# Packing the diagonal steps of causal attention into full score units

## The chip, the core and the metric

The kernel runs on one core of a Trainium2 chip. A core has five engines that run their own instruction streams and meet at semaphores: PE (TensorE, matrix products), DVE (VectorE) and ACT (ScalarE) for elementwise work, POOL (GpSimd), and SP, which here issues DMA transfers. PE writes only to PSUM, a small memory of eight banks of 128 partitions by 512 fp32 columns; the other tiles are in SBUF. The metric is the device time of one execution, in microseconds (us).

## The reference

Two transformer layers in a row; the change is in the attention of the first, over 4096 positions and 16 heads of 16 channels:

```python
scores = jnp.einsum('bhsd,bhtd->bhst', q, k) / math.sqrt(float(DH))
mask = jnp.tril(jnp.ones((S, S), dtype=scores.dtype))
scores = scores * mask
scores = jnp.where(scores == 0.0, -jnp.inf, scores)
attn = jax.nn.softmax(scores, axis=-1)
out = jnp.einsum('bhst,bhtd->bhsd', attn, v)
```

It is causal: query s sees keys t up to s. A score that is exactly 0 within the triangle is masked as well, so the kernel has to look at each score, not only at its place. Around it lie layer norms, the projections, a gated feed-forward, and in the second layer a linear-recurrence attention and a 16-expert feed-forward. None of that is touched.

## The kernel before

`phase_attend` does the attention as 32 blocks: 4 groups of 4 heads (g), and in each 8 blocks of 512 queries (j = 0 to 7). Block (g, j) has 4(j+1) steps, one for each tile of 128 keys (kt). A step's scores lie transposed, keys on partitions and queries along the columns. A step has two units, each of two heads: 128 x 1024 scores in two PSUM banks. `ps_s` holds three units.

For each unit PE makes the scores (L805, bf16), ACT takes exp of them into `probs` (L859), and DVE multiplies `probs` with "score is not 0" (L892, fp32), which also frees the unit's banks. In the second tile of every four below the diagonal ("shared" steps) one of the four heads goes another way: ACT copies its scores out (L864) and POOL does the comparison and the product (L904, L907). Then PE weighs the values of the whole step: four products of 32 output partitions, one for each head, in fp32 (L820), summed over the block's steps in `ps_o`. The sum of the weights comes with them as a further column of the values.

The last four steps of a block are the diagonal. In step d (0 to 3) only the queries from column 128 d on see its keys, so PE, ACT, DVE and the weighing work on 512, 384, 256 and 128 columns of each head (`w0 = 128 d`). In the first 128 of these columns, the square, the triangle cuts through: POOL sets what lies above it to 0 (L912, one instruction for the four heads), and the weighing waits for it (`masked`).

The order on PE is written out by hand: in step n it issues the scores of the step's second unit, then those of step n+1's first unit, then the weighing of step n-2. A unit's scores wait until DVE has done the unit three before (`bank`). `probs` has four slots, one for each step, so exp of step n waits for the weighing of step n-4. The end of block b is done inside block b+1's diagonal: ACT copies `ps_o` out in its step d=1 (L850), PE turns the copy over in step d=2 behind the weighing (L828, four transposes), and DVE normalises behind the last unit (L876 reciprocal, L880 product). Blocks with j = 0 do this a step later and leave normalising to the next block's first step. SP loads the queries of block b+1 as soon as the scores of block b-1 are all made (L755, eight transfers).

## Time and profile before

| | us |
|---|---|
| median of 3 runs | 2318.0 (2317.34 to 2320.04) |
| the profiled execution | 2317.24 |
| its span | 2315.5 |
| attention in it, first DVE instruction to last | 1286.87 (191.24 to 1478.11) |

Busy time over the span: PE 2003.0 us (87%), DVE 1665.2 (72%), ACT 1414.9 (61%), POOL 899.9 (39%). Such shares are means over stages with different limits. The page's row of tenths shows it: DVE at 9 in every slice from the fifth to the nineteenth, which is attention, and at 3 to 6 behind it. A group's "idle before" is time that the engine stood still just before these instructions, and what ended it. In a timeline each line has its start in us from the span's start, its length and its count. The next line can start a little before the end of the one before, since instructions of one engine overlap.

### The profile page before, as it was taken

Reading aid. Unit: us, or ns where it says so; the run is one execution under the profiler, and the core shown is the slowest. Engines: PE = TensorE matmul, PEld = TensorE weight load, DVE = VectorE, ACT = ScalarE, POOL = GpSimd, SP = SyncE. Lnnn points to the kernel's source line nnn. Section 1 sums busy time; section 2 is a strip of 40 time slices with the busy share of each in tenths; the row PEclk is TensorE's granted clock in tenths of the full one; section 3 lists DMA queues with packets and bytes.
Section 4 is the critical chain, followed back from the end, with each engine's and each line's share of the span. In section 5 each row is a group of like instructions: output and inputs, shape, how many; then the busy total and the mean of one; then the engine's idle time right before and its main releaser. Section 6 shows DMA issues by size and latency. Waiting matters only on the chain. (4 is left out here: it accounts for less than half of the span.)

```text
span 2315.5 us, 29427 instructions
## 1 busy us (share of the span) xinstructions
PE 2003.0 (87%) x10349; PEld 816.3 (35%) x10349; DVE 1665.2 (72%) x2280; ACT 1414.9 (61%) x1841; POOL 899.9 (39%) x777
## 2 busy tenths in 40 slices
PE   4986898988899988898989898678886699999997
PEld 4541111111111121111121111256553356767775
DVE  2776999999999999999999999556665544333332
ACT  0676888888888888888888888445554211111110
POOL 1682333333333333333333333126565174334334
PEclk8997999999999999999999999799998899999999
DMA  2463211102111112112530000110000043444441
GB/s 104 158 204 89 42 30 21 31 15 50 21 30 21 31 44 41 31 21 55 169 102 12 12 12 3 61 42 32 19 1 1 7 141 120 102 111 93 105 105 23
DMA packets 124646, 133.90 MB, mean 58 GB/s; under 512 B 35145, under 2 KB 118946, under 8 KB 123808
## 3 DMA queue, kind: packets, MB, share of 16 engines
q1 hardware_dynamic: 109920, 118.09, 18.9%
q0 software_dynamic: 14592, 14.08, 3.5%
q8 instruction: 77, 1.26, 0.2%
q14 instruction: 57, 0.47, 0.1%
HBM read 97.08 MB, written 50.63 MB: 64 GB/s over the span
## 5 line engine op out<-in xcount | busy, mean ns | idle before, releaser
L892 DVE SCALAR_TENSOR_TENSOR arena<-ps_s,arena 128x1024 f32<-128x1024 f32 (+3 forms) x1152 | 1163.1, 1076 | 114.5 <-ACT arena L859 108.1
L859 ACT ACTIVATE arena<-ps_s 128x1024 f32<-128x1024 f32 (+3 forms) x1152 | 1053.3, 959 | 192.7 <-PE ps_s L805 173.9
L805 PE MATMUL ps_s<-arena 128*128 128x512 bf16 (+3 forms) x2304 | 632.6, 367 | 145.1 <-DVE arena L892 98.8
L820 PE MATMUL ps_o<-arena,values 128*32 128x512 f32 (+3 forms) x4608 | 573.5, 570 | 0.4 <-POOL arena L912 0.4
L904 POOL TENSOR_SCALAR arena<-arena 128x512 f32<-128x512 f32 x112 | 215.0, 1919 | 611.1 <-ACT arena L864 611.1
L805 PEld LDWEIGHTS ps_s<-arena 128*128 128x128 bf16 x2304 | 143.1, 97 | 801.6 <-DVE arena L892 761.1
L1826 ACT ACTIVATE arena<-g_ps_g 128x320 f32<-128x320 f32 (+1 forms) x96 | 42.0, 438 | 311.0 <-PE g_ps_u L1760 311.0
L2011 POOL DMA_INDIRECT out<-values,slot_ids x80 | 123.8, 1547 | 240.7 <-DVE values L1975 212.4
L912 POOL TENSOR_SCALAR_AFFINE_SELECT arena<-arena 128x512 f32<-128x512 f32 x128 | 81.2, 635 | 239.2 <-DVE arena L892 239.2
L820 PEld LDWEIGHTS ps_o<-arena,values 128*32 128x32 f32 x4608 | 90.8, 108 | 224.8 <-issue 207.7
L1948 DVE TENSOR_TENSOR arena<-g_ps_u,arena 128x320 f32<-128x320 f32 (+1 forms) x96 | 47.2, 492 | 168.3 <-ACT arena L1826 168.3
L907 POOL TENSOR_TENSOR arena<-arena 128x512 f32<-128x512 f32 x112 | 142.6, 1274 | 9.3
L1253 PE MATMUL t_ps_out<-arena 128*128 128x256 f32 x512 | 126.8, 407 | 19.7 <-DVE arena L1483 8.8
L1760 PE MATMUL g_ps_g<-arena 128*128 128x320 f32 (+1 forms) x384 | 119.7, 434 | 0.6 <-issue 0.6
L1760 PE MATMUL g_ps_u<-arena 128*128 128x320 f32 (+1 forms) x384 | 120.1, 435 | 0.0
L1253 PEld LDWEIGHTS t_ps_out<-arena 128*128 128x128 f32 x512 | 103.7, 206 | 42.7 <-issue 19.9
L1775 PE MATMUL g_ps_d<-arena 128*128 128x256 f32 (+1 forms) x480 | 107.9, 381 | 1.1 <-DVE arena L1948 1.0
L1775 PEld LDWEIGHTS g_ps_d<-arena 128*128 128x128 f32 (+1 forms) x480 | 89.4, 189 | 15.3 <-DVE arena L1948 1.6
L1992 POOL DMA_INDIRECT slots_in_dram<-arena,scatter_at x64 | 70.3, 1099 | 55.0 <-issue 55.0
L1261 PE MATMUL t_ps_turn<-ident,arena 128*128 128x128 f32 x256 | 37.4, 294 | 52.2 <-ACT arena L1147 18.8
L1760 PEld LDWEIGHTS g_ps_u<-arena 128*128 128x128 f32 (+1 forms) x384 | 69.8, 182 | 34.5 <-issue 0.6
L1760 PEld LDWEIGHTS g_ps_g<-arena 128*128 128x128 f32 (+1 forms) x384 | 69.5, 181 | 33.2 <-issue 1.4
(201 smaller groups left out, 1780.7 us busy)
## 6 DMA issues: line engine op xcount, KB each, us to landing
arena<-parts_dram SPq DMA_DIRECT2D x320, 64.0 KB, 2.3
parts_dram<-arena SPq DMA_DIRECT2D x32, 384.0 KB, 2.9
arena<-parts_dram SPq DMA_DIRECT2D x24, 512.0 KB, 7.1
slots_in_dram<-in_empty_slots SPq DMA_DIRECT2D x10, 1040.0 KB, 25.5
arena<-slots_in_dram SPq DMA_DIRECT2D x16, 650.0 KB, 4.4
arena<-in_L_ffn_w_gate SPq DMA_DIRECT2D x16, 352.0 KB, 3.1
arena<-in_L_ffn_w_up SPq DMA_DIRECT2D x16, 352.0 KB, 3.7
arena<-in_L_attn_x SPq DMA_DIRECT2D x8, 512.0 KB, 3.9
```

The source lines that it names most:

```text
L805: last = pe.matmul(ps_s[:, u % 3, h, step.w0:], m.k_stack[:, head, step.kt * P:step.kt * P + P], q_stack[:, step.block % 2, 2 * pair + h, ...
L820: last = pe.matmul(ps_o[32 * h:32 * h + 32, step.block % 2, step.w0:], m.values_flat[:, at:at + 32], probs[:, step.slot, h, step.w0:], sta ...
L859: act.activation(probs[:, step.slot, 2 * pair:2 * pair + 2, step.w0:], ps_s[:, u % 3, :, step.w0:], ACT.Exp, scale=1.0 / DH ** 0.5).then_i ...
L892: dve.scalar_tensor_tensor(p, ps_s[:, u % 3, 0:heads, step.w0:], 0.0, p, ALU.not_equal, ALU.mult).then_inc(bank, 1)
L904: pool.tensor_scalar(s_copy, s_copy, 0.0, 0.0, ALU.is_equal, ALU.is_equal).then_inc(kept, 1)
L907: pool.tensor_tensor(p, p, s_copy, ALU.mult).then_inc(last_masked, 1)
L912: pool.affine_select(out=sq, in_=sq, compare_op=ALU.is_ge, fill=0.0, base=0, pattern=[[0, HG], [1, P]], channel_multiplier=-1).then_inc(ma ...
L1253: last = pe.matmul(ps_out[:, c, t * D:t * D + D], lhs[:, k, at:at + P], w[:, k], start=k == 0, stop=k == KC - 1)
L1760: last = pe.matmul(ps[0:rows_, n % 2, 0:HALF], w[:, s, k, at:at + rows_], inT[:, s, k, half * HALF:half * HALF + HALF], start=k == 0, stop ...
L1775: last = pe.matmul(ps_d[:, (s + i) % 2, at:at + D], hidden_e[0:rows_, s, f, c * P:c * P + P], w_down[0:rows_, s, f], start=f == 0, stop=f ...
L1992: pool.indirect_dma_start(out=m.slots_in[:, :], out_offset=bass.IndirectOffsetOnAxis(ap=m.scatter_at[:, k, t:t + 1], axis=0), in_=m.h_wide ...
L2011: pool.indirect_dma_start(out=out_rows, out_offset=bass.IndirectOffsetOnAxis(ap=ids[:, s, c:c + 1], axis=0), in_=rows_out[:, s, c], in_off ...
```

## The change

The four diagonal steps of a block, eight units of 1024, 768, 512 and 256 columns, become three steps with five units of 1024 columns each:

- "square": tile 4j, two full units, as step d=0 was.
- "mixed": tiles 4j+1 and 4j+3, two units. Each head's bank holds the 384 columns of the first and, in its last quarter, the 128 columns of the second.
- "half": tile 4j+2, one unit. The 256 columns of all four heads lie two to a bank.

The scores, exp and the product on DVE now always cover whole units. PE makes the same products as before, column for column, out of more places: the mixed step's unit takes four products (384, 384, 128, 128), the half step's takes four of 256. The weighing of the mixed step is eight instructions instead of four. POOL does two squares one after the other in the mixed step and one in each of the others, four in a block as before. A step now has one or two units, so units are counted on their own; the transposes stand in the half step, the copy in the mixed step (in the half step for j = 0), and normalising behind the half step's unit.

On PE the stretch around a diagonal (in a block with j = 2; the weighing of a step stands two steps behind its scores) read before:

```order
L820 MATMUL ps_o<-arena,values 32x512 x4
L805 MATMUL ps_s<-arena 128x384 x2
L805 MATMUL ps_s<-arena 128x256 x2
L820 MATMUL ps_o<-arena,values 32x512 x4
L805 MATMUL ps_s<-arena 128x256 x2
L805 MATMUL ps_s<-arena 128x128 x2
L820 MATMUL ps_o<-arena,values 32x512 x4
L828 MATMUL ps_o<-ident,arena 128x128 x4
L805 MATMUL ps_s<-arena 128x128 x2
L805 MATMUL ps_s<-arena 128x512 x2
L820 MATMUL ps_o<-arena,values 32x384 x4
L805 MATMUL ps_s<-arena 128x512 x4
```

and reads now:

```order
L853 MATMUL ps_o<-arena,values 32x512 x4
L836 MATMUL ps_s<-arena 128x384 x2
L836 MATMUL ps_s<-arena 128x128 x2
L836 MATMUL ps_s<-arena 128x256 x4
L853 MATMUL ps_o<-arena,values 32x512 x4
L836 MATMUL ps_s<-arena 128x512 x2
L853 MATMUL ps_o<-arena,values 32x512 x4
L861 MATMUL ps_o<-ident,arena 128x128 x4
L836 MATMUL ps_s<-arena 128x512 x4
L853 MATMUL ps_o<-arena,values 32x384 x4
L853 MATMUL ps_o<-arena,values 32x128 x4
L836 MATMUL ps_s<-arena 128x512 x4
```

The 384-column and 128-column scores of two steps have come together (second and third row), the half step's scores stand as four products in one unit, and between that unit and the transposes (L861) there are two weighings (rows with `ps_o<-arena,values`) with one pair of scores between them. The weighing of the mixed step is the pair of rows with 384 and 128 columns.

On DVE a block with j = 2 and the units of the next read before:

```order
L892 SCALAR_TENSOR_TENSOR arena<-ps_s,arena 128x1024 x7
L892 SCALAR_TENSOR_TENSOR arena<-ps_s,arena 128x512
L892 SCALAR_TENSOR_TENSOR arena<-ps_s,arena 128x1024 x6
L892 SCALAR_TENSOR_TENSOR arena<-ps_s,arena 128x2x384 x2
L892 SCALAR_TENSOR_TENSOR arena<-ps_s,arena 128x2x256 x2
L892 SCALAR_TENSOR_TENSOR arena<-ps_s,arena 128x2x128 x2
L876 RECIPROCAL arena<-ps_o 128x16
L880 TENSOR_TENSOR arena<-ps_o,arena 128x256
```

and read now:

```order
L926 SCALAR_TENSOR_TENSOR arena<-ps_s,arena 128x1024 x7
L926 SCALAR_TENSOR_TENSOR arena<-ps_s,arena 128x512
L926 SCALAR_TENSOR_TENSOR arena<-ps_s,arena 128x1024 x9
L910 RECIPROCAL arena<-ps_o 128x16
L914 TENSOR_TENSOR arena<-ps_o,arena 128x256
```

The six narrower products are gone, three full ones are there in their place (9 in a run, of which 5 are the diagonal's), and the normalising of the previous block stands behind the fifth.

The diff, without the lines that only follow from these:

```diff
+class Piece:
+
+
+    def __init__(self, head, kt, w0, bank, at, width):
+        self.head, self.kt, self.w0 = head, kt, w0
+        self.bank, self.at, self.width = bank, at, width
...
 class Step:
 
 
-    def __init__(self, n, g, j, kt):
-        self.n, self.g, self.j, self.kt = n, g, j, kt
+    def __init__(self, n, g, j, kind, kt, unit):
+        self.n, self.g, self.j, self.kind, self.kt = n, g, j, kind, kt
...
-        self.diag = kt - TT * j if kt >= TT * j else None
-        self.last = self.diag == TT - 1
-        self.w0 = P * self.diag if self.diag else 0
-        self.shared = self.diag is None and kt % 4 == 1
-
-    def unit(self, pair):
-
-        return 2 * self.n + pair
+        self.last = kind == "half"
+        self.shared = kind == "full" and kt % 4 == 1
+        self.pairs = 1 if kind == "half" else 2
+        self.unit = unit
+        self.squares = {"full": 0, "square": 1, "mixed": 2, "half": 1}[kind]
+
+    def pieces(self, pair):
+
+
+        if self.kind == "half":
+            return [Piece(h, self.kt, 2 * P, h // 2, h % 2 * 2 * P, 2 * P) for h in range(HG)]
+        heads = [(2 * pair + h, h) for h in range(2)]
+        if self.kind == "mixed":
+            return [Piece(head, self.kt, P, h, 0, 3 * P) for head, h in heads] + \
+                   [Piece(head, self.kt + 2, 3 * P, h, 3 * P, P) for head, h in heads]
+        return [Piece(head, self.kt, 0, h, 0, BT) for head, h in heads]
+
+    def last_unit(self):
+        return self.unit + self.pairs - 1
 
...
-        return self.block * TT + self.diag + 1
...
+        return self.block * TT + {"square": 0, "mixed": 1, "half": 3}[self.kind] + self.squares
...
+def block_kinds(j):
+
+    return [("full", kt) for kt in range(TT * j)] + [("square", TT * j), ("mixed", TT * j + 1), ("half", TT * j + 2)]
 
...
 BLOCKS = NG * NB
...
-    if step.diag == (1 if step.j else 2) and step.block:
+    if step.kind == ("mixed" if step.j else "half") and step.block:
         return step.block - 1
...
-    if step.diag == (2 if step.j else 3) and step.block:
+    if step.kind == "half" and step.block:
         return step.block - 1
...
-    if step.j and step.diag == 3:
+    if step.j and step.kind == "half":
         return step.block - 1
...
-                    sp.wait_ge(scored, 2 * steps_through(b - 2))
+                    sp.wait_ge(scored, units_through(b - 2))
...
-                for h in range(2):
-                    head = step.g % 2 * HG + 2 * pair + h
-                    last = pe.matmul(ps_s[:, u % 3, h, step.w0:], m.k_stack[:, head, step.kt * P:step.kt * P + P],
-                                     q_stack[:, step.block % 2, 2 * pair + h, step.w0:], start=True, stop=True)
+                for p in step.pieces(pair):
+                    last = pe.matmul(ps_s[:, u % 3, p.bank, p.at:p.at + p.width],
+                                     m.k_stack[:, step.g % 2 * HG + p.head, p.kt * P:p.kt * P + P],
+                                     q_stack[:, step.block % 2, p.head, p.w0:p.w0 + p.width], start=True, stop=True)
                 last.then_inc(scored, 1)
...
-                for h in range(HG):
-                    at = (step.kt * NH + step.g * HG + h) * (DH + 1)
-                    last = pe.matmul(ps_o[32 * h:32 * h + 32, step.block % 2, step.w0:], m.values_flat[:, at:at + 32],
-                                     probs[:, step.slot, h, step.w0:], start=step.first, stop=step.last,
-                                     tile_position=(0, 32 * h))
+                pieces = [(pair, p) for pair in range(step.pairs) for p in step.pieces(pair)]
+                for pair, p in sorted(pieces, key=lambda entry: (entry[1].kt, entry[1].head)):
+                    at = (p.kt * NH + step.g * HG + p.head) * (DH + 1)
+                    last = pe.matmul(ps_o[32 * p.head:32 * p.head + 32, step.block % 2, p.w0:p.w0 + p.width],
+                                     m.values_flat[:, at:at + 32], probs[:, step.slot, 2 * pair + p.bank, p.at:p.at + p.width],
+                                     start=step.first, stop=step.last, tile_position=(0, 32 * p.head))
                 last.then_inc(probs_free, 1)
...
-                    score(step, 1)
+                    if step.pairs == 2:
+                        score(step, 1)
...
-                    for pair in range(2):
-                        u = step.unit(pair)
+                    for pair in range(step.pairs):
+                        u = step.unit + pair
                         act.wait_ge(scored, u + 1)
-                        act.activation(probs[:, step.slot, 2 * pair:2 * pair + 2, step.w0:], ps_s[:, u % 3, :, step.w0:], ACT.Exp,
+                        act.activation(probs[:, step.slot, 2 * pair:2 * pair + 2], ps_s[:, u % 3], ACT.Exp,
                                        scale=1.0 / DH ** 0.5).then_inc(exped, 1)
...
-                    for pair in range(2):
-                        u = step.unit(pair)
+                    for pair in range(step.pairs):
+                        u = step.unit + pair
                         dve.wait_ge(exped, u + 1)
...
-                        p = probs[:, step.slot, 2 * pair:2 * pair + heads, step.w0:]
-                        dve.scalar_tensor_tensor(p, ps_s[:, u % 3, 0:heads, step.w0:], 0.0, p, ALU.not_equal, ALU.mult).then_inc(bank, 1)
...
-                    if step.diag is not None:
-
-                        pool.wait_ge(bank, step.unit(1) + 1)
-                        sq = probs[:, step.slot, :, step.w0:step.w0 + P]
-                        pool.affine_select(out=sq, in_=sq, compare_op=ALU.is_ge, fill=0.0, base=0,
-                                           pattern=[[0, HG], [1, P]], channel_multiplier=-1).then_inc(masked, 1)
+                    if step.squares:
+
+                        pool.wait_ge(bank, step.last_unit() + 1)
+                        if step.kind == "half":
+                            heads = probs[:, step.slot, 0:2].rearrange("p b (h n) -> p (b h) n", h=2)
+                        else:
+                            heads = probs[:, step.slot]
+                        for c in range(step.squares):
+                            sq = heads[:, :, 3 * P * c:3 * P * c + P]
+                            pool.affine_select(out=sq, in_=sq, compare_op=ALU.is_ge, fill=0.0, base=0,
+                                               pattern=[[0, HG], [1, P]], channel_multiplier=-1).then_inc(masked, 1)
```

## Rows read from the trace of the kernel before

**Rows 1.** Busy time by stretch: one diagonal, one block with j = 0, all of attention.

```profile
core 0: us, PE busy (x) PEld busy (x) DVE busy (x) ACT busy (x) POOL busy (x), PEclk, DMA share, GB/s
1011.06:1018.76 7.70, 7.22 (x54) 2.10 (x53) 6.71 (x12) 5.79 (x9) 2.54 (x4) 1.00 0.04 10
512.75:520.11 7.36, 5.78 (x51) 1.85 (x50) 6.13 (x9) 5.80 (x9) 2.54 (x4) 1.00 0.34 90
191.24:1478.11 1286.87, 1150.86 (x7036) 245.64 (x7034) 1181.85 (x1216) 1105.67 (x1295) 438.85 (x352) 1.00 0.17 38
```

**Rows 2.** Waits of DVE from 209 to 1467 us: total, times, longest.

```profile
DVE arena L892 <- ACT arena L859: 91.8, 145, 0.8
```

**Rows 3.** Groups by shape, DVE, 209 to 1467 us.

```profile
L892 DVE SCALAR_TENSOR_TENSOR arena<-ps_s,arena 128x1024 f32<-128x1024 f32 x838 | 964.5, 1217 | 73.1 <-ACT arena L859 69.9
L892 DVE SCALAR_TENSOR_TENSOR arena<-ps_s,arena 128x512 f32<-128x512 f32 x171 | 116.5, 683 | 2.9
L892 DVE SCALAR_TENSOR_TENSOR arena<-ps_s,arena 128x768 f32<-128x768 f32 x60 | 54.4, 948 | 0.0
L892 DVE SCALAR_TENSOR_TENSOR arena<-ps_s,arena 128x256 f32<-128x256 f32 x60 | 25.2, 420 | 22.0 <-ACT arena L859 22.0
```

**Rows 4.** Timeline of DVE over that diagonal: start, length, instruction, count [idle before].

```profile
1011.06 1.22 DVE L892 SCALAR_TENSOR_TENSOR arena<-ps_s,arena 128x1024 f32<-128x1024 f32 x1
1012.19 1.22 DVE L892 SCALAR_TENSOR_TENSOR arena<-ps_s,arena 128x1024 f32<-128x1024 f32 x1
...
1017.62 0.42 DVE L892 SCALAR_TENSOR_TENSOR arena<-ps_s,arena 128x256 f32<-128x256 f32 x1 [0.76 <-ACT arena L859]
1017.97 0.25 DVE L876 RECIPROCAL arena<-ps_o 128x16 f32<-128x16 f32 x1
1018.25 0.43 DVE L880 TENSOR_TENSOR arena<-ps_o,arena 128x256 f32<-128x256 f32 x1
1018.76 1.23 DVE L892 SCALAR_TENSOR_TENSOR arena<-ps_s,arena 128x1024 f32<-128x1024 f32 x1
1020.02 1.23 DVE L892 SCALAR_TENSOR_TENSOR arena<-ps_s,arena 128x1024 f32<-128x1024 f32 x1
```

**Rows 5.** Timeline of PE over it.

```profile
1013.46 0.39 PE L805 MATMUL ps_s<-arena 128*128 128x256 bf16 x2 [0.34 <-DVE arena L892]
...
1015.41 1.06 PE L820 MATMUL ps_o<-arena,values 128*32 128x512 f32 x8
1016.40 0.66 PE L828 MATMUL ps_o<-ident,arena 128*128 128x128 f32 x4
...
1021.30 0.60 PE L805 MATMUL ps_s<-arena 128*128 128x512 bf16 x2 [0.66 <-DVE arena L892]
1021.83 0.43 PE L820 MATMUL ps_o<-arena,values 128*32 128x128 f32 x8
```

**Rows 6.** Timeline of ACT and POOL over it.

```profile
1013.87 0.59 ACT L850 ACTIVATE arena<-ps_o 128x512 f32<-128x512 f32 x1
...
1013.48 0.63 POOL L912 TENSOR_SCALAR_AFFINE_SELECT arena<-arena 128x512 f32<-128x512 f32 x1 [4.54 <-DVE arena L892]
```

**Rows 7.** Timeline of DVE behind the diagonal of a block with j = 0.

```profile
521.85 1.23 DVE L892 SCALAR_TENSOR_TENSOR arena<-ps_s,arena 128x1024 f32<-128x1024 f32 x1 [0.52 <-ACT arena L859]
```

**Rows 8.** Timeline of SP: loads of queries at the start and in the diagonal.

```profile
191.02 10.59 SPq L755 DMA_DIRECT2D arena<-parts_dram  x16
...
1017.20 3.62 SPq L755 DMA_DIRECT2D arena<-parts_dram  x8
```

**Rows 9.** The page, issues to the DMA queues: KB each, us to landing.

```profile
arena<-parts_dram SPq DMA_DIRECT2D x320, 64.0 KB, 2.3
```

**Rows 10.** Timeline of PE in the first block.

```profile
195.71 1.94 PE L820 MATMUL ps_o<-arena,values 128*32 128x512 f32 x8
```

**Rows 11.** The page, costliest groups: POOL's other pass, and the weight loads of scores.

```profile
L904 POOL TENSOR_SCALAR arena<-arena 128x512 f32<-128x512 f32 x112 | 215.0, 1919 | 611.1 <-ACT arena L864 611.1
...
L805 PEld LDWEIGHTS ps_s<-arena 128*128 128x128 bf16 x2304 | 143.1, 97 | 801.6 <-DVE arena L892 761.1
```

More of the change, by code:

```diff
@@ L811, in weigh @@
                     pe.wait_ge(o_ready, step.block - 1)
-                if step.diag is None:
-                    pe.wait_ge(bank, step.unit(1) + 1)
+                if step.kind == "full":
+                    pe.wait_ge(bank, step.last_unit() + 1)
                     if step.shared:
@@ L863, in _ @@
                             act.wait_ge(last_masked, step.shares())
-                        act.activation(s_copy, ps_s[:, step.unit(1) % 3, 1], ACT.Copy).then_inc(scores_out, 1)
+                        act.activation(s_copy, ps_s[:, step.last_unit() % 3, 1], ACT.Copy).then_inc(scores_out, 1)
                     if copied_in(step) is not None:
@@ L902, in _ @@
                         pool.wait_ge(scores_out, step.shares() + 1)
-                        pool.wait_ge(exped, step.unit(1) + 1)
+                        pool.wait_ge(exped, step.last_unit() + 1)
                         pool.tensor_scalar(s_copy, s_copy, 0.0, 0.0, ALU.is_equal, ALU.is_equal).then_inc(kept, 1)
```

26 lines of the change are left out of this document (16 added, 10 removed).

## The prediction

> **What bounds the kernel now.** I read the page's shares first, then busy time by stretch. Attention is 1286.87 us of the span, and in it DVE is busy 1181.85 us (92%), PE 1150.86 and ACT 1105.67 [rows 1]; a pipelined PE's busy time is not its limit, so DVE is the engine to follow. Its waits come next: 91.8 us in 145 waits, all on ACT's exp [rows 2], and the groups by shape say where: 69.9 us of waits stand before full units, 22.0 us before the 60 units of the last diagonal step, with 256 elements [rows 3]. Last I read a diagonal engine by engine (block j = 5 of the third group; its first unit on DVE starts at 1011.06, called 0 below). A diagonal takes 7.70 us from its first unit to the next block's first, with DVE busy 6.71 us [rows 1]; of the 27 such diagonals before the last one, 26 take 7.70 and one 7.98.
>
> In that stretch DVE starts full units every 1.13 us though each lasts 1.22 [rows 4], so an instruction in a stream costs its duration less 0.087. Eight units then make 2 x (1.217 + 0.948 + 0.683 + 0.420) - 8 x 0.087 = 5.84 us [rows 3]. The last unit waits 0.76 us for ACT; normalising (from 1017.97 to the next unit at 1018.76) takes 0.79 [rows 4]; the remaining 0.3 is small gaps. The wait of 0.76 comes from PE: the scores of that unit stand behind a weighing and four transposes, 1015.41 to about 1016.90 [rows 5].
>
> **What the change does to DVE.** It takes away three instructions and no element: five full units cost 5 x 1.13 = 5.65 us, only 0.19 less than 5.84. Dropped whole, at the fixed part of their rows (1217 less twice the step from 256 to 512 elements is about 0.15 each), they would look like 0.45, but most of that is already hidden by overlap [rows 3, 4].
>
> The Trainium skill's page "VectorE: DVE Perf Modes" (section on the TRN2 errata) gives each instruction that reads PSUM 120 cycles beside its elements, exposed between instructions. That is an estimate of 0.125 us each, 0.375 a block, and 12 us over 32 blocks; the rows here give 0.19 and 6 us. Neither is the result, since the wait that ends last lies on PE.
>
> **What it does to PE, where the end of a diagonal is set.** The columns of scores and weighing are the same. What changes is what is late. In time from the first unit:
> - 2.40: the half step's scores may start. They wait for DVE's second unit, exactly as the pair at 1013.46 does now, whose place in the ring of three they take [rows 5].
> - +0.53: a unit of 1024 columns until the weighing behind it starts (1021.30 to 1021.83) [rows 5]: 2.93
> - +0.99: weighing of the last full step (1015.41 to 1016.40) [rows 5]: 3.92
> - +0.53: scores of the next block's first unit, free to go since the mixed step's first unit is done at 2.26 + 1.22 = 3.48: 4.45
> - +0.99: weighing of the square step; its square is set by POOL from about 2.42 for 0.63 us, as now at 1013.48 [rows 6]: 5.44
> - +0.66: the transposes [rows 5]: 6.10
> - +0.06, then 0.28 from reciprocal to product and 0.51 from product to the next unit [rows 4]: 6.95.
>
> So the next block starts at 6.95 instead of 7.70, a gain of 0.75. DVE's own side is earlier: the half unit's exp follows the mixed step's second exp (about 2.3 to 3.34) and the copy, about 0.5 more in a stream [rows 6], and DVE does it from 4.77 to 5.99, before the 6.16 at which the transposes let the reciprocal go. So 0.5 us of the 7.70's idle time stays.
>
> Then the next unit. Now the block's second unit starts 1.26 behind its first, having waited for exp [rows 4]. In the new order its scores come straight behind the transposes, at about 5.95 to 6.55, and exp is over by 7.6, while DVE is in the first until 8.17: 1.13 behind, 0.13 gained.
>
> **The other edits.** POOL's two squares of the mixed step start when DVE has done its second unit, 4.61: 4.67 + 2 x 0.63 + 0.08 = 6.0. PE comes to that weighing at about 6.95, so 0.9 us of cover; behind the waiting weighing stand the second step's scores, for which ACT and DVE would wait. The weighing of eight instructions I take at 1.14 (between 0.99, if the second four run beside the first, and 1.28, the sum of the two busy times), at no cost: PE is done by 8.24 at the latest, when the next scores, which wait for DVE's 8.17, may start. The load of queries takes 3.62 us to issue and 2.3 to land [rows 8, 9], about 6 from the half unit's scores, while the block with j = 0 behind it gives more than 7: hidden. Four slots of `probs` for three diagonal steps keep exp behind a weighing that is two us old. What attention gives up is given up by the whole program, since the next phase waits for all engines at a barrier.
>
> **Blocks with j = 0** do not normalise in the diagonal: 7.36 now [rows 1], then another 521.85 - 520.11 = 1.74 to the second unit [rows 7], 9.10 in all. In the new order DVE runs its five units through, 5.65, and the second unit of the next block then waits: scores of the half unit at 2.42, weighing of 256 columns (about 0.57), scores once DVE is through the third unit at 3.49, weighing and transposes bring PE to about 5.6, +0.6 scores, +1.02 exp, so 7.3. Gain 1.8.
>
> **The sum.** 27 diagonals (28 with j of 1 or more, less the last) x 0.75 = 20.3. The second unit, 24 x 0.13 = 3.1 (three of the 27 are followed by a block with j = 0). Three j = 0 blocks inside, 3 x 1.8 = 5.4. The very first block can gain at most 1.7: its successor's queries are issued from 191.02, 3.62 long, and land 2.2 later [rows 8, 9]; and PE runs there at half pace, 1.94 for a weighing [rows 10], so I take 1.2 for blocks 0 and 1 beyond what is counted. The tail behind the last diagonal, 0.3. Together 30.3. 2317.24 - 30.3 = 2286.9 for the profiled execution; the median of the runs lies 0.8 above it, so the forecast is 2287.7.
>
> **Bounds.** The unknown is the four weight loads in one unit. A load is 97 ns [rows 11], a 256-column product about 107 (half of what a 512-column pair's spacing gives), so in the half unit loads hide; a 128-column product is about 53, so a load behind it sticks out by some 0.04. If none hid, a unit would take 4 x 0.097 longer: 0.39 in the half unit, and another 0.6 by way of the mixed units, about 1.0 a block, which would eat 27 us. I take the nearest row, the pair of full products, and 0. Below: if switching between scores and weighing cost nothing in the new places, about 0.1 three times a block, 8 us more gained.
>
> The Trainium skill's page "TensorE: Matmul & The Clock Gate" (section LDWEIGHTS) gives a load one cycle of 1.2 GHz for each column, 107 ns for 128, more than a 128-column product takes at the full clock. It speaks against the mixed step. The row says 97 ns, overlapped with the product in front.
>
> **Rivals.**
> 1. DVE stays the bound throughout: the transposes come in time, the diagonal is 5.65 + 0.79 = 6.44. For it: PE's steps above are taken from places where it had just waited. Against: two weighings between the half unit and the transposes, each 0.99. Time: 27 x 0.51 = 14 us less, 2274. Chance 0.06.
> 2. Weight loads or the eight-part weighing show on PE, 0.1 to 0.9 us a block: 2290 to 2312, middle 2299. For: the chain above has no slack from 2.93 on. Against: LDWEIGHTS overlaps everywhere in the trace. Chance 0.14, a fifth of it within 0.2% of no change.
> 3. Slower: POOL's squares. If the select over shifted columns ran at the pace of POOL's other pass over as many elements, 1.92 us instead of 0.63 [rows 11], the mixed step's pair would end at 8.6, 1.6 behind PE's arrival; the second step's scores would come 1.5 late and DVE about 1.3, more than the 0.88 gained: 27 x 0.4 = 11 us slower, 2328. It decides once each select takes over 1.5 us. Against: the same operation on 512 elements, 0.63 each time. Chance 0.03.
> 4. Nothing is gained because another wait takes all of it back further on in the block (the full steps have a wait of 0.7 each four): 2318, chance 0.03. Against: that wait is made anew every four steps and does not depend on how the block began.
>
> The forecast has 0.74. A measurement of this kernel can tell about 0.2%, 4.6 us. Faster by more than that: 0.74 + 0.06 + 0.11 = 0.91 and a little; within: 0.05; slower: 0.03. The forecast's own range is 2282 to 2293; with rivals 1 and 2 the range of 8 in 10 is 2279 to 2299.
>
> **What would show it.** A diagonal of 6.9 to 7.0 us on DVE with five units of about 1.22 us and no narrow ones; the reciprocal waiting for the transposes, not for exp; the next block's second unit 1.13 behind its first; j = 0 blocks 5.65 long with a wait of about 0.5 behind; POOL's pair of selects done before PE gets to that weighing. The half unit's scores showing more than 0.53 to the weighing behind them, or a wait of PE for POOL in every block, would prove me wrong.

## The result and the profile after

| | before | changed |
|---|---|---|
| median, us | 2318.09 (4 runs, 2317.34 to 2320.04) | 2284.32 (4 runs, 2280.82 to 2288.65) |
| ratio, 95% interval | | 0.9854 (0.9832 to 0.9876) |
| the profiled execution, its span | 2317.24, 2315.5 | 2288.65, 2286.9 |
| attention in it | 1286.87 | 1253.69 |
| behind attention in it | 837.4 | 841.4 |

The kernel is 1.5% faster, 33.8 us by the medians; 30.3 were forecast (2287.7). The profiled execution of the changed kernel is its slowest of four. Its attention is 33.2 us shorter, and what follows attention is 4 us longer, with TensorE's granted clock at the lower of its two levels (1.2 GHz) for 100 us of it against 89 before. One later execution of the changed kernel, at a mean granted clock of 0.56 instead of 0.97, took 3261 us and is left out of all that follows. Busy time by stretch, for the same three stretches as in [rows 1]:

```profile
core 0: us, PE busy (x) PEld busy (x) DVE busy (x) ACT busy (x) POOL busy (x), PEclk, DMA share, GB/s
989.88:996.68 6.80, 6.56 (x47) 2.29 (x46) 6.43 (x9) 5.49 (x7) 2.50 (x4) 1.00 0.18 58
506.34:512.00 5.66, 5.03 (x50) 2.01 (x49) 5.66 (x7) 5.19 (x6) 1.62 (x3) 1.00 0.41 112
191.86:1445.55 1253.69, 1135.29 (x7036) 256.70 (x7034) 1169.93 (x1120) 1093.09 (x1199) 437.64 (x352) 1.00 0.17 39
```

The diagonal of the same block (third group, j = 5) takes 6.80 us instead of 7.70, and a block with j = 0 is 5.66 long, as forecast, with DVE never idle in it. DVE's busy time in attention fell by only 12 us; the other 21 were waits.

DVE's waits from 209 to 1430 us (us in all, times, longest):

```profile
DVE arena L926 <- ACT arena L893: 71.8, 137, 0.7
DVE arena L910 <- PE ps_o L861: 4.0, 26, 0.2
```

and its products by shape over the same stretch (busy, mean ns | idle before):

```profile
L926 DVE SCALAR_TENSOR_TENSOR arena<-ps_s,arena 128x1024 f32<-128x1024 f32 x924 | 1061.2, 1217 | 71.9 <-ACT arena L893 71.8
L926 DVE SCALAR_TENSOR_TENSOR arena<-ps_s,arena 128x512 f32<-128x512 f32 x110 | 74.9, 681 | 0.0
```

Full units last 1217 ns as before [rows 3], the narrow shapes are gone with the 22.0 us of waits before the narrowest, and there is a new small wait, of the reciprocal for PE's transposes. What stays, 72 us, is mostly a wait of 0.7 us (84 times) in every fourth full step.

The diagonal on DVE (start, length, instruction, count [idle before]), then on PE, then on ACT and POOL. The profile has each fp32 product of the weighing as two records, so x8 is a weighing of four products and x16 the mixed step's eight:

```profile
989.88 1.22 DVE L926 SCALAR_TENSOR_TENSOR arena<-ps_s,arena 128x1024 f32<-128x1024 f32 x1
991.01 1.22 DVE L926 SCALAR_TENSOR_TENSOR arena<-ps_s,arena 128x1024 f32<-128x1024 f32 x1
...
994.66 1.23 DVE L926 SCALAR_TENSOR_TENSOR arena<-ps_s,arena 128x1024 f32<-128x1024 f32 x1 [0.18 <-ACT arena L893]
996.04 0.26 DVE L910 RECIPROCAL arena<-ps_o 128x16 f32<-128x16 f32 x1 [0.15 <-PE ps_o L861]
996.34 0.42 DVE L914 TENSOR_TENSOR arena<-ps_o,arena 128x256 f32<-128x256 f32 x1
996.68 1.21 DVE L926 SCALAR_TENSOR_TENSOR arena<-ps_s,arena 128x1024 f32<-128x1024 f32 x1
997.81 1.22 DVE L926 SCALAR_TENSOR_TENSOR arena<-ps_s,arena 128x1024 f32<-128x1024 f32 x1
```

```profile
991.55 1.33 PE L836 MATMUL ps_s<-arena 128*128 128x384 bf16 x8
992.82 1.07 PE L853 MATMUL ps_o<-arena,values 128*32 128x512 f32 x8
993.82 0.60 PE L836 MATMUL ps_s<-arena 128*128 128x512 bf16 x2
994.35 1.07 PE L853 MATMUL ps_o<-arena,values 128*32 128x512 f32 x8
995.35 0.66 PE L861 MATMUL ps_o<-ident,arena 128*128 128x128 f32 x4
995.84 1.03 PE L836 MATMUL ps_s<-arena 128*128 128x512 bf16 x4
996.80 1.07 PE L853 MATMUL ps_o<-arena,values 128*32 128x384 f32 x16
997.95 0.61 PE L836 MATMUL ps_s<-arena 128*128 128x512 bf16 x2
```

```profile
993.12 0.59 ACT L884 ACTIVATE arena<-ps_o 128x512 f32<-128x512 f32 x1
993.60 1.95 ACT L893 ACTIVATE arena<-ps_s 128x1024 f32<-128x1024 f32 x2
```

```profile
994.55 1.23 POOL L951 TENSOR_SCALAR_AFFINE_SELECT arena<-arena 128x512 f32<-128x512 f32 x2 [1.62 <-DVE arena L926]
```

Counted from 989.88, the weighing before the next block's scores is on PE at 2.94, those scores at 3.94, the square step's weighing at 4.47, the transposes at 5.47 to 6.13 and the reciprocal at 6.16; forecast were 2.93, 3.92, 4.45, 5.44, 6.10 and 6.16. The weighing of eight products takes 1.07 us, not longer than one of four products of 512 columns. POOL's pair of selects is over at 5.90 and PE comes to that weighing at 6.92, a cover of 1.0.

In the first block PE waits for the queries of the second, as its timeline has it (the idle time before a row in brackets):

```profile
197.25 1.04 PE L836 MATMUL ps_s<-arena 128*128 128x512 bf16 x2 [2.36 <-DMA arena<-parts_dram]
198.21 1.94 PE L853 MATMUL ps_o<-arena,values 128*32 128x512 f32 x8
```

### The profile page after: what moved, and what is told of

The parts are those of the page before. It is cut to its first block and busy times, and to the rows that moved or that the text cites. A ratio compares the mean times of both kernels' runs of the same rounds, so it can differ in the third digit from the quotient of the medians.

```text
span 2286.9 us, 29203 instructions
## 1 busy us (share of the span) xinstructions
PE 1989.9 (87%) x10349; PEld 829.1 (36%) x10349; DVE 1651.6 (72%) x2184; ACT 1402.7 (61%) x1745; POOL 898.8 (39%) x777
## 3 DMA queue, kind: packets, MB, share of 16 engines
q8 instruction: 77, 1.26, 0.2%
## 5 line engine op out<-in xcount | busy, mean ns | idle before, releaser
L926 DVE SCALAR_TENSOR_TENSOR arena<-ps_s,arena 128x1024 f32<-128x1024 f32 (+1 forms) x1056 | 1151.0, 1160 | 88.7 <-ACT arena L893 88.6
L893 ACT ACTIVATE arena<-ps_s 128x1024 f32<-128x1024 f32 x1056 | 1040.2, 1030 | 171.0 <-PE ps_s L836 156.9
L836 PE MATMUL ps_s<-arena 128*128 128x512 bf16 (+3 forms) x2304 | 620.4, 366 | 127.4 <-DVE arena L926 76.8
L853 PE MATMUL ps_o<-arena,values 128*32 128x512 f32 (+3 forms) x4608 | 566.5, 569 | 0.5 <-POOL arena L951 0.5
L836 PEld LDWEIGHTS ps_s<-arena 128*128 128x128 bf16 x2304 | 151.0, 97 | 754.1 <-DVE arena L926 675.9
L1389 ACT ACTIVATE arena<-t_ps_turn,mod_cols 128x512 f32<-128x512 f32 x48 | 34.8, 775 | 75.6 <-PE t_ps_turn L1300 75.6
```

Source lines behind the costliest of these rows:

```text
L836: last = pe.matmul(ps_s[:, u % 3, p.bank, p.at:p.at + p.width], m.k_stack[:, step.g % 2 * HG + p.head, p.kt * P:p.kt * P + P], q_stack[:, ...
L853: last = pe.matmul(ps_o[32 * p.head:32 * p.head + 32, step.block % 2, p.w0:p.w0 + p.width], m.values_flat[:, at:at + 32], probs[:, step.sl ...
L893: act.activation(probs[:, step.slot, 2 * pair:2 * pair + 2], ps_s[:, u % 3], ACT.Exp, scale=1.0 / DH ** 0.5).then_inc(exped, 1)
L926: dve.scalar_tensor_tensor(p, ps_s[:, u % 3, 0:heads], 0.0, p, ALU.not_equal, ALU.mult).then_inc(bank, 1)
```

## The experiments

Lengths of attention are from each kernel's profile, from its first DVE product to the end of its last normalising. They repeat well: two profiles of the changed kernel gave 1253.69 and 1254.65. Whole executions of one kernel spread more, those of the kernel before over up to 10 us (2312.3 to 2322.2 in one set). The experiments were timed in three sets, and each ratio is to the kernel before in the same set. Kernels with one execution are judged by their profile alone. In a block with j of 1 or more, "diagonal" is the time from its first diagonal unit on DVE to the next block's first unit, "second unit" the time from there to the one behind.

| | diagonal | second unit | attention | median, us (runs) | ratio to before |
|---|---|---|---|---|---|
| before | 7.70 | 1.26 | 1286.9 | 2316.8, 2317.5, 2320.4 (17, 15, 9) | |
| changed, again | 6.80 | 1.13 | 1254.65 | 2283.0 (4) | 0.985 (0.9833 to 0.9866) |
| only the shared banks | 7.60 | 1.13 | 1280.2 | 2309.0 (6) | 0.9964 (0.9951 to 0.9978) |
| only the half unit | 7.50 | 1.26 | 1285.0 | 2312.8 (12) | 0.9978 (0.9968 to 0.9987) |
| transposes first | 6.55 | 1.13 | 1249.2 | 2279.4 (5) | 0.9836 (0.982 to 0.9852) |
| before, transposes late | 7.36 | 1.70 | 1290.3 | 2320.2 (10) | 1.0009 (0.9998 to 1.002) |
| selects doubled | 6.80 | 1.13 | 1264.8 | 2292.9 (1) | |
| selects tripled | 6.80 | 1.13 | 1309.3 | 2341.9 (1) | |
| square units split | 6.93 | 1.13 | 1258.3 | 2289.1 (1) | |
| half unit split | 6.80 | 1.13 | 1253.7 | 2284.4 (1) | |
| three moves | 6.33 | 1.13 | 1247.9 | 2280.1 (5) | 0.984 (0.9822 to 0.9858) |
| three moves and a later weighing | 6.33 | 1.13 | 1247.8 | 2276.0 (5) | 0.9811 (0.9795 to 0.9826) |

**The changed kernel again.** No edit.

> The changed kernel once more, unaltered, beside the others. My theory: all of the gain lies in attention, whose first to last DVE instruction took 1286.9 us before and 1253.7 in the first profile of the changed kernel, 33.2 less, and this repeats to within 0.5 us (diagonals of 6.80). The runs of the changed kernel spread over 2281 to 2289; if that comes from the phases behind attention, the profile here has the same 1253.7 and the rest of the span differs by up to 7 us. Rival: attention itself varies from run to run, then its length differs here by some us.

Measured: attention 1254.65, 1.0 off rather than 0.5; it comes from the full steps of the second block, block 1 (11.65 us against 10.31), in which the granted clock was at its lower level until 201.85 instead of 200.04, and every diagonal of a block with j of 1 or more is as before. Behind attention it took 836.1 us, against 841.4 in the first profile. So the spread lies behind attention. It goes with the clock there: over all thirteen profiles, TensorE's granted clock was at its lower level for 85 to 92 us in the nine in which that stretch took 835.0 to 837.8 us, and for 95 to 100 us in the four in which it took 840.1 to 841.4. No run varied the clock by itself.

**Each part alone.** The lists of steps are, for the shared banks, and for the half unit:

```diff
-    return [("full", kt) for kt in range(TT * j)] + [("square", TT * j), ("mixed", TT * j + 1), ("half", TT * j + 2)]
+    return [("full", kt) for kt in range(TT * j)] + [("square", TT * j), ("mixed", TT * j + 1), ("narrow", TT * j + 2)]
```

```diff
-    return [("full", kt) for kt in range(TT * j)] + [("square", TT * j), ("mixed", TT * j + 1), ("half", TT * j + 2)]
+    return [("full", kt) for kt in range(TT * j)] + [("square", TT * j), ("narrow", TT * j + 1), ("half", TT * j + 2), ("narrow", TT * j + 3)]
```

"narrow" is a step of two units on the visible columns, as before the change. The previous block's sums are copied out in tile 4j+1's step, turned over in tile 4j+2's and normalised in the last, whatever their kinds (blocks with j of 1 or more); other lines follow from this.

> One part alone: tiles 1 and 3 of the diagonal share banks, tile 2 stays two narrow units of 512 elements. Theory (the end of a diagonal is set by PE's queue behind the ring of three units): scores of the next block's first unit now wait for the mixed step's second unit, free at 4.61, so 4.67 + 0.53 + 0.99 (weighing) + 0.66 (transposes) and normalising give a diagonal of about 7.5 us, 0.17 less than the 7.70 before; with the second unit 0.13 closer and the j = 0 blocks, 12 to 14 us less than before in all, 2305. Rival (DVE's count of instructions and the gaps beside each): two of the three instructions removed, two thirds of the gain, diagonal 7.1, 2296.

> The other part alone: tile 2 of the diagonal is one unit of the four heads, tiles 1 and 3 stay narrow. Theory: weighing to 3.93, scores of the last narrow step's first unit, weighing to 5.14, transposes, then the last narrow unit and the next block's first scores at 5.75, whose exp ends at 7.40: diagonal 7.44, 0.26 less than before, and the second unit 1.3 behind; in all 8 to 10 us less than before, 2309. Rival (instructions removed, one of three): a third of the gain, diagonal 7.4 too, 2307. So this run does not tell the two apart by itself; the sum of the two parts does: theory 0.43 of the 0.90 that both together give, rival all of it.

Measured: diagonals of 7.60 and 7.50, where 7.5 and 7.44 were expected. The parts give 0.10 and 0.20, together 0.30, where both at once give 0.90 and the theory had 0.43. Neither a third for each instruction removed nor a gain for each gap fits that. The times were missed by more, 2309.0 and 2312.8 instead of 2305 and 2309: attention is 6.7 and 1.8 us shorter. With the half unit alone, the 27 diagonals give 5.7 us, and the full steps of the three later blocks with j = 1 take back 4.0 of it (11.21 us each instead of 9.88). That goes with the clock, not with the order on PE: in each of them TensorE's granted clock is at its lower level for 3.4 us (from 522.48, 843.33 and 1164.18), in the first after PE had stood 0.84 and 0.79 us waiting for DVE. PE's timeline has the weighing in it:

```profile
522.43 1.88 PE L842 MATMUL ps_s<-arena 128*128 128x512 bf16 x4 [0.79 <-DVE arena L932]
524.23 1.86 PE L859 MATMUL ps_o<-arena,values 128*32 128x512 f32 x8
```

The kernel before has no such stretch behind its first block. With the shared banks alone there is one (from 835.72), across two blocks that took 1.6 us more than their like.

The timeline of DVE with the shared banks alone has the reciprocal at

```profile
1014.96 0.26 DVE L916 RECIPROCAL arena<-ps_o 128x16 f32<-128x16 f32 x1 [1.17 <-PE ps_o L867]
```

and that of PE before it reads

```profile
1011.71 0.39 PE L842 MATMUL ps_s<-arena 128*128 128x256 bf16 x2
1012.75 0.59 PE L842 MATMUL ps_s<-arena 128*128 128x512 bf16 x2 [0.64 <-DVE arena L932]
1013.27 1.07 PE L859 MATMUL ps_o<-arena,values 128*32 128x512 f32 x8
1014.26 0.66 PE L867 MATMUL ps_o<-ident,arena 128*128 128x128 f32 x4
```

DVE's stream is shorter here and then stands 1.17 us before the reciprocal. With six units instead of five, the next block's scores need the mixed step's second unit, not its first, so PE stands 0.64 us and the weighing and the transposes come behind that.

With the half unit alone it is another chain. The last narrow unit is still there, so the next block's first scores stand behind the transposes on PE, as before the change. ACT's timeline has the exps of these two units, and DVE's the next block's first:

```profile
1014.94 1.52 ACT L899 ACTIVATE arena<-ps_s 128x256 f32<-128x256 f32 x2 [1.25 <-PE ps_s L842]
```

```profile
1016.49 1.23 DVE L932 SCALAR_TENSOR_TENSOR arena<-ps_s,arena 128x1024 f32<-128x1024 f32 x1
```

That exp ends at 1016.46 and DVE starts at 1016.49. Only with five units are the next block's scores clear of both: they wait for the mixed step's first unit alone, and stand ahead of the transposes. It is this place that both parts together win.

**Order on PE in the changed kernel.** The transposes go ahead of the square step's weighing:

```diff
+                    if turned_in(step) is not None and step.j:
+                        turn_over(turned_in(step))
                     if step.n >= 2:
                         weigh(steps[step.n - 2])
-                    if turned_in(step) is not None:
+                    if turned_in(step) is not None and not step.j:
                         turn_over(turned_in(step))
```

> The changed kernel with PE's four transposes of the previous block before the square step's weighing instead of behind it (blocks with j of 1 or more). Theory: the transposes are the last to come in the diagonal; they then end at 5.14, the half unit's product on DVE at 6.02 is last, and the diagonal is 6.57 instead of 6.81; the second unit's scores come as before, so 0.24 x 27 = 6.5 us less than the changed kernel, 2278. Rival (the end is set by DVE's own stream or by exp of the next unit): no change, 2284.

Measured: 6.55, and DVE runs through, as its timeline shows:

```profile
990.37 1.23 DVE L928 SCALAR_TENSOR_TENSOR arena<-ps_s,arena 128x1024 f32<-128x1024 f32 x1 [0.18 <-ACT arena L895]
991.51 0.25 DVE L912 RECIPROCAL arena<-ps_o 128x16 f32<-128x16 f32 x1
991.79 0.42 DVE L916 TENSOR_TENSOR arena<-ps_o,arena 128x256 f32<-128x256 f32 x1
992.13 1.21 DVE L928 SCALAR_TENSOR_TENSOR arena<-ps_s,arena 128x1024 f32<-128x1024 f32 x1
```

No wait stands before the reciprocal any more. So the transposes did end the diagonal of the changed kernel. Attention is 5.5 us shorter than in the changed kernel's second profile (4.5 than in its first), of the 6.5 expected: the full steps behind took 0.06 more a block.

**Order on PE in the kernel before.**

```diff
+                    if step.j and step.block and step.diag == 3:
+                        turn_over(step.block - 1)
                     if step.n >= 2:
                         weigh(steps[step.n - 2])
-                    if turned_in(step) is not None:
+                    if turned_in(step) is not None and not step.j:
                         turn_over(turned_in(step))
```

> The kernel before the change, with PE's transposes moved from the third diagonal step to the fourth, behind the scores of its last unit and of the next block's first, and ahead of the weighing (blocks with j of 1 or more). Theory: in the old order the last narrow unit and the next block's first unit came late because their scores stood behind the transposes; now their scores start at 5.34 instead of 5.84, exp of the next unit ends at 7.1, the transposes end at 6.65, normalising lets DVE go on at 7.3: diagonal 7.3 instead of 7.70, 27 x 0.4 = 10 us less, 2307. Rival (the old end was set by normalising alone, 0.51 from product to next unit whatever comes before): diagonal 7.5, 2312.

Measured: the diagonal fell to 7.36, near the 7.3 expected, and the kernel did not get 10 us faster but stayed the same; attention is 3.5 us longer. What the expectation left out is the next unit. PE's timeline, and DVE's:

```profile
1017.48 0.60 PE L828 MATMUL ps_o<-ident,arena 128*128 128x128 f32 x4
1018.01 0.85 PE L820 MATMUL ps_o<-arena,values 128*32 128x384 f32 x8
1018.79 1.04 PE L805 MATMUL ps_s<-arena 128*128 128x512 bf16 x4
```

```profile
1018.80 1.23 DVE L894 SCALAR_TENSOR_TENSOR arena<-ps_s,arena 128x1024 f32<-128x1024 f32 x1
1020.49 2.95 DVE L894 SCALAR_TENSOR_TENSOR arena<-ps_s,arena 128x1024 f32<-128x1024 f32 x3 [0.47 <-ACT arena L861]
```

The second unit's scores come behind transposes and weighing at 1018.79, so DVE starts it 1.70 behind the first. The wait had only moved by one unit. The diagonals of the three later blocks with j = 0 also became longer, 7.79, 7.79 and 8.74 instead of 7.36; in the last of them the granted clock was at its lower level for 3.4 us (from 1160.32). The packing gains where this order doesn't, because it leaves less before the second unit's scores: they start 5.97 us after the diagonal's first unit, against 7.26 in the kernel before and 7.36 here.

**POOL's cover.** Each select of the mixed step is done twice, or (with `range(2 ...`) three times; the further ones change nothing (the diff leaves out the declarations of `again_sem` and `extra`):

```diff
                         for c in range(step.squares):
                             sq = heads[:, :, 3 * P * c:3 * P * c + P]
+                            for again in range(1 if step.kind == "mixed" else 0):
+                                pool.affine_select(out=sq, in_=sq, ...).then_inc(again_sem, 1)
+                                extra += 1
+                                pool.wait_ge(again_sem, extra)
                             pool.affine_select(out=sq, in_=sq, ...).then_inc(masked, 1)
```

> The changed kernel with each of POOL's two selects of the mixed step done twice (the second time changes nothing), to use up the time between POOL's end (5.91) and PE's arrival at that weighing (6.93). Theory: four selects end at about 7.4, the weighing waits 0.5 us, the second step's scores come 0.4 late, which exp just bears, but the unit behind the copy of the shared scores is then 0.4 late: 27 x 0.4 = 11 us slower than the changed kernel. Rival (the cover is larger, since DVE has slack further on): no change in the length of attention, 1254 us.

> The same with each select done three times. Theory: six selects end at about 8.9, 2.0 us behind PE's arrival, and the delay passes on one to one: 1.5 at the second step's second unit and 1.9 behind the copy, 27 x 1.9 = 51 us more than the changed kernel's 1254 us of attention, slower than the kernel before (1287). With a run of 1254 to 1265 the slower rival of the prediction would have been priced too high.

Measured: attention 1264.8 and 1309.3, against 1265 and 1305 expected. With the selects tripled, PE's timeline in the same block, and its waits for POOL from 209 to 1430 us:

```profile
1032.13 1.07 PE L854 MATMUL ps_o<-arena,values 128*32 128x384 f32 x16 [1.77 <-POOL arena L958]
1033.14 1.04 PE L837 MATMUL ps_s<-arena 128*128 128x512 bf16 x4
```

```profile
PE ps_o L854 <- POOL arena L958: 54.9, 30, 2.4
```

The diagonals stay at 6.80, and the cost is in the full steps behind. With the selects doubled PE waits 0.37 us for POOL in this block and a block's full steps take 0.29 more; with them tripled it waits 1.77 and they take 1.69 more. So there is about 1 us of cover, and beyond it 1.40 us more of waiting cost 1.40 us more. The rival that ended on the slower side, with 1.6 us behind PE's arrival, was priced about right. It did not happen because a select over shifted columns takes the same 0.63 us.

**What a DVE instruction costs.** The product of each of the square step's units, or (with `"half"` in the first line) that of the half unit, is cut in two:

```diff
+                        if step.kind == "square":
+                            for h in range(2):
+                                p = probs[:, step.slot, 2 * pair + h:2 * pair + h + 1]
+                                last = dve.scalar_tensor_tensor(p, ps_s[:, u % 3, h:h + 1], 0.0, p, ALU.not_equal, ALU.mult)
+                            last.then_inc(bank, 1)
+                            continue
```

> The changed kernel with both DVE products of the square step cut into two of 512 elements each, two instructions more in a block at the head of the diagonal. Theory by the stream interval (1.13 for 1024 elements, so 0.064 beside the elements): DVE's second unit ends 0.13 later, the half unit's scores wait for it, and the diagonal is 6.93 instead of 6.80; 1254 + 3.6 = 1258 us of attention. Rival by the fixed part of the duration (0.15 each): 7.1, 1262 us.

> The changed kernel with the half unit's DVE product cut into two of 512 elements, one instruction more just before normalising. Theory (the diagonal ends with PE's transposes, DVE stands 0.15 idle before its reciprocal): the unit ends 0.06 later and nothing else moves in blocks with j of 1 or more, diagonal 6.80, attention 1254 us; in the three blocks with j = 0 0.06 each at most. Rival (DVE's stream ends it): 6.86, 1256 us.

Measured: 6.93 and 6.80, attention 1258.3 and 1253.7, both as the theory had them. An instruction more costs 0.065 us where the chain runs over DVE (the head of the diagonal) and nothing where it runs over PE.

**Going further.** Three moves in blocks with j of 1 or more: the copy goes between the mixed step's two exps, the transposes behind the next block's first scores, and the square step's weighing behind its second:

```diff
                         act.activation(probs[...], ps_s[:, u % 3], ACT.Exp, ...).then_inc(exped, 1)
+                        if pair == 0 and step.j and copied_in(step) is not None:
+                            copy_out(copied_in(step))
...
-                    if copied_in(step) is not None:
+                    if copied_in(step) is not None and not step.j:
                         copy_out(copied_in(step))
...
                         score(step, 1)
+                    before = steps[step.n - 1] if step.n else None
+                    if before and before.kind == "half" and before.j:
+                        weigh(steps[step.n - 3])
                     if step.n + 1 < len(steps):
                         score(steps[step.n + 1], 0)
+                    late = step.kind == "half" and step.j and step.n + 1 < len(steps)
+                    if turned_in(step) is not None and step.j:
+                        turn_over(turned_in(step))
-                    if step.n >= 2:
+                    if step.n >= 2 and not late:
                         weigh(steps[step.n - 2])
-                    if turned_in(step) is not None:
+                    if turned_in(step) is not None and not step.j:
                         turn_over(turned_in(step))
```

> The changed kernel with three moves, in blocks with j of 1 or more: ACT copies the previous block's sums between the two exps of the mixed step, PE turns them over right behind the scores of the next block's first unit, and the square step's weighing comes behind the scores of that block's second unit. Theory: with the transposes out of the way (that alone gave a diagonal of 6.55) DVE still stood 0.18 before the half unit, because the copy delayed its exp; now the half unit starts at 4.58 on DVE and the diagonal is 6.34, against 6.80 for the changed kernel, and nothing of it comes back, as the second unit's scores are 1 us earlier: 27 x 0.46 = 12.4 less, perhaps 2 of them given back where the third unit waits for the mixed weighing; 2272. Rival: the second unit or the weighing behind it becomes late and returns the gain, then 2277 to 2280.

Measured: the diagonal is 6.33, but the full steps behind it take 0.28 us more (46.43 instead of 46.15 in a block with j = 5), and attention is 1247.9, 6 to 7 us less than the changed kernel's instead of 10 to 12. The expectation placed what would come back in the third unit; it came back at the shared step, whose copy and the exp behind it wait for scores that PE has made at 8.49, as with the transposes first (8.48). The rival had the time (2280.1; it said 2277 to 2280) but not the place: the second unit is not late (1.13).

**And a later weighing of the mixed step**, behind the second step's second unit. `late` then holds for the step after the half step too, and the step after that does both weighings.

> The kernel with the three moves, and the mixed step's weighing moved too, behind the scores of the second step's second unit. Reason: with the three moves the diagonal fell to 6.33 but the full steps behind it took 0.28 us more; the first wait in them is for exp behind the shared scores' copy, whose input PE makes only at 8.48, with no idle time on PE since 2.40. Theory (PE's queue is now the limit up to the shared step): those scores come at 7.60 to 8.20, the weighing ends at 9.2, the scores behind it end at 9.73 and exp of that unit starts 0.16 earlier; 24 x 0.16 = 4 us less attention than with the three moves, 1244 us. Rival (the gap of every fourth step re-forms whatever comes before it): attention stays at 1248 us.

Measured: 46.35 in that block, 0.08 less where 0.16 was expected, and 0.33 more in the diagonals of three blocks with j = 0; attention is 1247.8, the same, as the rival said. The runs of this kernel were the fastest (2274.9 to 2277.3). In its profile the stretch behind attention took 836.5 us, against 840.1 with the three moves alone, with the granted clock at its lower level for 86.5 against 95.5 us; by attention the two are equal. What is shown for both is an attention 6 to 7 us shorter than the changed kernel's, 0.3% of the whole; that the later weighing is faster than the three moves alone is not.

## Why the prediction was right

The sum, term by term, against the profile:

| term | forecast | measured |
|---|---|---|
| 27 diagonals | 20.3 | 24.4 |
| second units (24 blocks) | 3.1 | 2.9 |
| three blocks with j = 0 and what follows | 5.4 | 5.3 |
| blocks 0 and 1 | 1.2 | 0.05 |
| tail | 0.3 | 0.7 |
| attention | 30.3 | 33.2 |

The measured terms are sums of the block lengths on DVE before and after: (26 x 7.70 + 7.98) less (26 x 6.80 + 6.94), 24 x 0.12, 3 x 1.77, and so on; they add to within 0.2 of the whole. The 33.2 us are an error of +4.1 in the diagonals and one of -1.2 in blocks 0 and 1. That the profiled execution came within 2 us of its forecast (2288.65, forecast 2286.9) is luck: its attention was 3 us shorter than forecast and what follows 4 us longer.

**The chain over PE** was right in every step but the last, to 0.03 us. That it decides is shown by the transposes moved ahead (6.55), by the half unit split without effect, and by the two parts alone. Of the rest, the second unit 1.13 behind the first, the 5.66 of a block with j = 0 and the cover of POOL came as forecast.

**The term that was mis-sized** is "0.51 from product to the next unit", taken from [rows 4]. In the kernel before, that unit did not wait for normalising but for its own exp, as ACT's timeline has it:

```profile
1017.21 1.51 ACT L859 ACTIVATE arena<-ps_s 128x256 f32<-128x256 f32 x2 [1.12 <-PE ps_s L805]
```

The row counts two exps (the last narrow unit and the next block's first, named by the first shape). They end at 1018.72, and DVE starts at 1018.76. In the changed kernel exp is long done (993.60 + 1.95 = 995.55), and the unit follows the product after 0.34 us (996.34 to 996.68). That makes 6.80 instead of 6.95, and 27 x 0.15 = 4 us. I had given a wait behind a chain the length of the chain.

**Blocks 0 and 1.** The bound by the queries held (PE waits 2.36 us for them, the block is 7.51 instead of 8.74), but PE's slow weighing of 1.94 then stands before the next scores. The granted clock is at its lower level until 200.04, with block 1 begun at 199.37; in the kernel before it was until 199.03, with block 1 begun at 199.98. So the full steps of block 1 gave back almost all of the gain (10.31 us instead of 9.13): its second unit came 2.40 behind the first.

**DVE's instructions.** The 0.19 us for three instructions fewer was right as a cost in a stream: two more cost 0.13. It was wrong as a fall of busy time, 6 us in all: that fell by 11.9. The durations in attention fell by 14.4 us, 0.15 for each of the 96 instructions gone, but the overlaps by only 2.5, since DVE now stands still less often and more of its instructions follow directly. The fixed part itself was worded wrongly: 0.15 is 1217 less twice the step from 512 to 1024 elements, not from 256 to 512 [rows 3]. The Trainium skill's page "VectorE: DVE Perf Modes" (section on the TRN2 errata) gives 120 cycles beside the elements, an estimate of 0.125 us each, twice what the splits show here. Its 12 us over 32 blocks agree with the fall of busy time, though not with the cost in a stream.

**Weight loads.** Four loads in one unit cost nothing that can be seen. PE's timeline has a mixed unit and the weighing behind it, then the half unit and its own:

```profile
990.02 0.61 PE L836 MATMUL ps_s<-arena 128*128 128x384 bf16 x4
990.56 0.64 PE L853 MATMUL ps_o<-arena,values 128*32 128x512 f32 x4
```

```profile
992.28 0.61 PE L836 MATMUL ps_s<-arena 128*128 128x256 bf16 x4
992.82 0.64 PE L853 MATMUL ps_o<-arena,values 128*32 128x512 f32 x4
```

Either unit is 0.54 us ahead of its weighing, against 0.53 for two products of 512 columns [rows 5]. The Trainium skill's page "TensorE: Matmul & The Clock Gate" (section LDWEIGHTS) gives a load 107 ns, an estimate from its one cycle of 1.2 GHz for each of 128 columns, twice as long as a 128-column product; by these rows a load shows no more beside such products than beside wide ones.

**The rivals.** DVE as the bound throughout was wrong for the changed kernel and nearly right once the order on PE was changed too (6.33, against 6.44 foreseen). The slower rival had about the right price and the wrong select. The second rival cost nothing (0.54 for four loads, 1.07 for the weighing of eight products). Its own range, 2290 to 2312, lies wholly more than 4.6 us below 2318, so a fifth of it could not be "within 0.2% of no change"; the chance of a faster kernel was about 0.94 by its own numbers.

## What to carry to other kernels

Where several engines pass units around a ring, count how many units stand between a late instruction and the place it waits for: two edits that each take units away gave 0.10 and 0.20 us a block alone and 0.90 together. When an end is read off a row, look at what else ended there; a unit that starts 0.04 us behind its exp is waiting for exp, whatever stands before it on its own engine. And a shorter stretch is worth what reaches the next fixed wait: twice here a diagonal 0.3 to 0.5 us shorter gave part or all of that back in the next unit or in the shared step behind.

## What the runs showed of the hardware

Within attention, 3.4 us with TensorE's granted clock at 1.2 instead of 2.4 GHz cost the block 1.33 us (the half unit alone, three times: 11.21 instead of 9.88). Behind attention, 11 us more at the lower level came with 4 us more time (before and changed, first profiles).

Eight fp32 products of 32 output partitions, four of 384 and four of 128 columns, take 1.07 us together, as long as four of 512 columns, and where nothing holds them the next scores start 1.01 us behind their start (1032.13 to 1033.14 with the selects tripled); I had expected 1.14, up to 1.28 as a bound. Two selects on POOL without a wait between them overlap a little, 1.23 us for the pair rather than the 1.34 that I had put.
